# The first feed-forward of a four-layer perceiver: seven program blocks made one, weights quantised as one tile, transposes turned four to a bank and copied by ScalarE

## The chip, the cores and the metric

The kernel runs on one core of a Trainium2 chip (trn2). The metric is the device time of one execution in microseconds (us). Before the change the median of three runs is 4526.8 us.

## The reference, cut to what matters

Twelve stages (cross attention, attention and a feed-forward network, four times over) each add to `x`, of shape (16, 64, 128): 1024 rows of 128 values. The change touches the third stage alone, in which rows and weights are rounded to a 4-bit float grid in groups of 16, each with its own scale:

```python
def fp4_quant_dequant(x):
    xb = x.reshape(shape[:-1] + (shape[-1] // 16, 16))
    scale = jnp.maximum(jnp.max(jnp.abs(xb), axis=-1, keepdims=True) / 6.0, 1e-12)
    xn = xb / scale
    idx = jnp.searchsorted(_MID, jnp.abs(xn))
    return (_GRID[idx] * jnp.sign(xn) * scale).reshape(shape)
...
gate = fp4_linear(x, w_gate)      # w_gate, w_up: (352, 128)
y = fp4_linear(x, w_up)
h = jax.nn.silu(gate) * y         # (rows, 352)
return fp4_linear(h, w_down)      # w_down: (128, 352)
...
x = x + _L0_ffn_ref(_layernorm(x, axis=-1), L0_ffn_w_gate, L0_ffn_w_up, L0_ffn_w_down)
```

`fp4_linear` quantises both of its operands and multiplies them.

## The kernel before

Each stage is a function, and `perceiver` calls the twelve one after the other. A stage is written as program blocks (`nc.Block()`): in a block each engine has a list of instructions of its own, ordered against the other engines by semaphores, and all engines meet in a barrier at the block's end. After a stage `end_stage` lets GpSimd (POOL) clear every semaphore that the stage used and raise it by one again; GpSimd does this alone, ahead of its part of the next stage's first block, while the other engines go on to that block.

`x` lies in SBUF as 8 row tiles of 128 rows by 128 values (NT is 8). `layernorm` is one block: SyncE (SP) issues the stage's loads (`loads`, line 157) and waits for them; VectorE (DVE) makes `c.xn`; TensorE (PE) and ScalarE (ACT) make a transposed copy; GpSimd fills what stands in `fills` (line 168). The block ends when all of that is done.

`stage_l0_ffn`, the feed-forward, is seven blocks before the change:

1. `layernorm`, with seven loads: the gate and up weights in three pieces each (128, 128 and 96 rows by 128 values), and the down weights (128 by 352).
2. `quantize_all` of the rows (128 by 1024), the down weights (128 by 352) and the six pieces. `quantize` is 13 VectorE instructions, each of which waits for the one before it through `Link`.
3. `turn_all` of 17 tiles: TensorE transposes one tile into one of two PSUM buffers (line 236), VectorE copies it out (line 243).
4. For each row tile `t` two matmuls of 352 columns (lines 2887 and 2888) into `pg` and `pu`, two buffers each; ScalarE takes Silu of `pg` (line 2895), VectorE multiplies it with `pu` (line 2901) into `h`.
5. `quantize_all` of `h` (128 by 2816).
6. `turn_all` of the 24 tiles of `h`.
7. The down projection, 24 matmuls into `py` (line 2912), and one addition to `x` (line 2918).

A float32 matmul stands as two instructions in the profile, a transpose as one.

Of the kernel before, what the change touches and what calls it, by code (L numbers as in the profile page):

```python
# [5 lines left out]
ALU = mybir.AluOpType  # L6
ACT = mybir.ActivationFunctionType
# [7 lines left out]
B, S, D = 16, 64, 128  # L15
NT = B * S // 128
# [11 lines left out]
ONE = 1  # L28
# [77 lines left out]
def bc(ap, shape):  # L106
    return ap.to_broadcast(shape)
# [115 lines left out]
def turn_all(c, jobs):  # L223

    nc = c.nc
    with ExitStack() as st:
        pt = [c.ps(st, f"turn{j}", [128, 512]) for j in range(2)]
        turned, copied = c.sem("turned"), c.sem("turn_copied")
        with nc.Block() as block:
            @block.tensor  # L230
            def _(pe):
                for n, (out, src) in enumerate(jobs):
                    if n >= 2:
                        pe.wait_ge(copied, n - 1 + ONE)
                    p, f = src.shape
                    pe.transpose(pt[n % 2][0:f, 0:p], src, c.ident[0:p, 0:p]).then_inc(turned, 1)

            @block.vector
            def _(dve):
                for n, (out, src) in enumerate(jobs):  # L240
                    p, f = src.shape
                    dve.wait_ge(turned, n + 1 + ONE)
                    dve.tensor_copy(out, pt[n % 2][0:f, 0:p]).then_inc(copied, 1)
                dve.wait_ge(copied, len(jobs) + ONE)
# [2574 lines left out]
def quantize(dve, link, v, a, q, b, s, r):  # L2819

    shape = list(v.shape)
    ai, qi, vi = a.bitcast(I32), q.bitcast(I32), v.bitcast(I32)
    link(dve.tensor_reduce(s[:, :, 0], v, X, ALU.max, apply_absolute_value=True))
    link(dve.tensor_scalar(s, s, 1.0 / 12.0, 0.5e-12, ALU.mult, ALU.max))
    link(dve.reciprocal(r, s))
    link(dve.tensor_tensor(v, v, bc(r, shape), ALU.mult))
    link(dve.tensor_scalar(ai, vi, 0x7FFFFFFF, None, ALU.bitwise_and))
    link(dve.tensor_scalar(qi, ai, 0x7F800000, None, ALU.bitwise_and))  # L2830
    link(dve.scalar_tensor_tensor(out=q, in0=q, scalar=0.25 - 2.0 ** -23, in1=a, op0=ALU.mult, op1=ALU.add))
    link(dve.tensor_scalar(qi, qi, 0x7FC00000, None, ALU.bitwise_and))
    link(dve.tensor_scalar(b, a, 0.5, -2.0, ALU.is_gt, ALU.add))
    link(dve.scalar_tensor_tensor(out=b, in0=a, scalar=1.5, in1=b, op0=ALU.is_gt, op1=ALU.add))
    link(dve.scalar_tensor_tensor(out=q, in0=q, scalar=2.0, in1=b, op0=ALU.max, op1=ALU.add))
    link(dve.scalar_tensor_tensor(out=vi, in0=vi, scalar=SIGN, in1=qi, op0=ALU.bitwise_and, op1=ALU.bitwise_or))
    link(dve.tensor_tensor(v, v, bc(s, shape), ALU.mult))


def stage_l0_ffn(c):  # L2840
    nc, d = c.nc, c.dram
    I = 352
    IC = [(0, 128), (128, 128), (256, 96)]
    with ExitStack() as st:
        wT = c.sb(st, "wT", [128, 2, I])
        wdT = c.sb(st, "wdT", [128, 3, D])
        h = c.sb(st, "h", [128, NT, I])
        u = c.sb(st, "u", [128, NT, I])
        a = c.sb(st, "a", [128, NT * I // 16, 16])
        q = c.sb(st, "q", [128, NT * I // 16, 16])  # L2850
        b = c.sb(st, "b", [128, NT * I // 16, 16])
        s = c.sb(st, "s", [128, NT * I // 16, 1])
        r = c.sb(st, "r", [128, NT * I // 16, 1])
        xqT = c.sb(st, "xqT", [128, NT, 128])
        hT = c.sb(st, "hT", [128, 3, NT, 128])
        w = c.sb(st, "w", [128, 2, 3, D])
        wd = c.sb(st, "wd", [128, I])
        wl = [(w[0:n, g, k, :], d[name][o:o + n, :]) for g, name in enumerate(("L0_ffn_w_gate", "L0_ffn_w_up"))
              for k, (o, n) in enumerate(IC)]
        layernorm(c, wl + [(wd[:], d["L0_ffn_w_down"])])  # L2860

        def quantize_all(parts):
            order = c.sem("quant_order")
            with nc.Block() as block:
                @block.vector
                def _(dve):
                    link = Link(dve, order)
                    for v in parts:
                        p, n = v.shape[0], v.shape[1]
                        quantize(dve, link, v, a[0:p, 0:n, :], q[0:p, 0:n, :], b[0:p, 0:n, :], s[0:p, 0:n, :], r[0:p, 0:n, :])  # L2870

        quantize_all([c.xn[:].rearrange("p t (n b) -> p (t n) b", b=16), wd[:].rearrange("p (n b) -> p n b", b=16)]
                     + [v.rearrange("p (n b) -> p n b", b=16) for v, _ in wl])
        turn_all(c, [(xqT[:, t, :], c.xn[:, t, :]) for t in range(NT)]
                 + [(wT[:, g, o:o + n], w[0:n, g, k, :]) for g in range(2) for k, (o, n) in enumerate(IC)]
                 + [(wdT[0:n, k, :], wd[:, o:o + n]) for k, (o, n) in enumerate(IC)])
        with ExitStack() as s2:
            pg = c.ps(s2, "pg", [128, 2, 512])
            pu = c.ps(s2, "pu", [128, 2, 512])
            made, silu, used = c.sem("made"), c.sem("silu"), c.sem("used")  # L2880
            with nc.Block() as block:
                @block.tensor
                def _(pe):
                    for t in range(NT):
                        if t >= 2:
                            pe.wait_ge(used, t - 1 + ONE)
                        pe.matmul(pg[:, t % 2, 0:I], xqT[:, t, :], wT[:, 0, :], start=True, stop=True)
                        pe.matmul(pu[:, t % 2, 0:I], xqT[:, t, :], wT[:, 1, :], start=True, stop=True
                                  ).then_inc(made, 1)

                @block.scalar
                def _(act):
                    for t in range(NT):
                        act.wait_ge(made, t + 1 + ONE)
                        act.activation(u[:, t, :], pg[:, t % 2, 0:I], ACT.Silu).then_inc(silu, 1)

                @block.vector
                def _(dve):
                    for t in range(NT):
                        dve.wait_ge(silu, t + 1 + ONE)  # L2900
                        dve.tensor_tensor(h[:, t, :], u[:, t, :], pu[:, t % 2, 0:I], ALU.mult).then_inc(used, 1)
                    dve.wait_ge(used, NT + ONE)
        quantize_all([h[:].rearrange("p t (n b) -> p (t n) b", b=16)])
        turn_all(c, [(hT[0:n, k, t, :], h[:, t, o:o + n]) for k, (o, n) in enumerate(IC) for t in range(NT)])
        py = c.ps(st, "py", [128, NT, D])
        summed, added = c.sem("summed"), c.sem("added")
        with nc.Block() as block:
            @block.tensor
            def _(pe):
                for t in range(NT):  # L2910
                    for k, (o, n) in enumerate(IC):
                        last = pe.matmul(py[:, t, :], hT[0:n, k, t, :], wdT[0:n, k, :], start=(k == 0), stop=(k == 2))
                last.then_inc(summed, 1)

            @block.vector
            def _(dve):
                dve.wait_ge(summed, 1 + ONE)
                dve.tensor_tensor(c.x[:], c.x[:], py[:], ALU.add).then_inc(added, 1)
                dve.wait_ge(added, 1 + ONE)


BIG = 1.0e30
# [189 lines left out]
def align(c, dcol, dist):  # L3112
# [8 lines left out]
    with ExitStack() as st:  # L3121
# [300 lines left out]
        with nc.Block() as block:  # L3422
# [57 lines left out]


STAGES = [stage_l0_xattn, stage_l0_attn, stage_l0_ffn, stage_l1_xattn, stage_l1_attn, stage_l1_ffn, stage_l2_xattn,
          stage_l2_attn, stage_l2_ffn, stage_l3_xattn, stage_l3_attn, stage_l3_ffn]

# [34 lines left out]
```

## Time and profile before

| | us |
|---|---|
| median of three runs (4524.62 to 4530.95) | 4526.8 |
| the profiled execution's own time | 4532.81 |
| its span in the trace | 4531.1 |
| busy in the span: TensorE matmul | 3534.2 |
| VectorE | 3437.9 |
| ScalarE | 2802.6 |
| GpSimd | 1035.8 |

Span is from the first to the last recorded event of the profiled execution; every time in the rows below counts from its start. The changed stage takes from 557.7 us to 680.1 us in it. The busy sums are over twelve stages that follow one another, so they say nothing about one stage.

### The profile page before, as it was taken

What the parts mean: (1) busy time and instruction counts of PE and PEld (TensorE: products, weight loads), DVE (VectorE), ACT (ScalarE), POOL (GpSimd) and SP (SyncE); (2) the same over time, 40 slices, a digit from 0 to 9 for tenths busy, and PEclk for the clock granted to TensorE, in tenths of its full rate; (3) what the DMA queues carried; (4) which work ended last, traced back from release to release, by engine and by line L of the source; (5) the groups of instructions that cost most, each with busy time, mean ns of one, the idle gap of its engine ahead of it and who ended that gap; (6) DMA issues with size and microseconds to landing.
All of it is one profiled execution on the core that took longest, in us unless ns stands there. A gap on an engine that the chain in (4) does not pass through costs nothing. (4 is left out here: it accounts for less than half of the span.)

```text
span 4531.1 us, 71930 instructions
## 1 busy us (share of the span) xinstructions
PE 3534.2 (78%) x25855; PEld 2837.7 (63%) x25855; DVE 3437.9 (76%) x5581; ACT 2802.6 (62%) x4626; POOL 1035.8 (23%) x1054
## 2 busy tenths in 40 slices
PE   6345638999999677999999875777777777777786
PEld 3334316999998555899999752555555555555574
DVE  4775776777777622877788657999999999999643
ACT  3113505666666423666666534999989998999732
POOL 0000402111210201121111001444444344443310
PEclk9556758999999888999999987999999999999887
DMA  8652001101100101010010001000000000000000
GB/s 273 95 97 67 6 0 64 44 31 37 37 30 16 26 24 62 30 44 30 30 39 28 22 5 39 15 15 21 24 15 15 15 30 15 15 15 8 20 4 17
DMA packets 186565, 161.25 MB, mean 36 GB/s; under 512 B 8220, under 2 KB 174316, under 8 KB 186220
## 3 DMA queue, kind: packets, MB, share of 16 engines
q1 hardware_dynamic: 182828, 142.83, 11.9%
q10 hardware_dynamic: 3392, 13.93, 0.9%
q8 instruction: 203, 3.33, 0.3%
q14 instruction: 142, 1.16, 0.1%
HBM read 127.36 MB, written 20.20 MB: 33 GB/s over the span
## 5 line engine op out<-in xcount | busy, mean ns | idle before, releaser
L538 PEld LDWEIGHTS psU<-ctxN,ST 128*128 128x128 f32 x6656 | 853.8, 191 | 98.1 <-issue 39.2
L538 PE MATMUL psU<-ctxN,ST 128*128 128x129 f32 x6656 | 868.0, 275 | 20.5 <-issue 20.5
L1160 DVE MAX8 top<-pairs 128x8 f32<-128x801 f32 (+1 forms) x512 | 709.2, 1406 | 4.5
L624 ACT ACTIVATE ST<-ST 128x512 f32<-128x512 f32 (+1 forms) x832 | 513.2, 625 | 166.8 <-DVE ST L726 162.5
L1125 POOL TENSOR_TENSOR P<-P,EX 128x1601 f32<-128x1601 f32 x128 | 459.8, 3592 | 580.0 <-ACT P L1035 580.0
L935 PE MATMUL psU<-ctxN,PT 128*128 128x129 f32 (+1 forms) x3328 | 432.6, 281 | 202.5 <-ACT PT L1043 202.5
L726 DVE TENSOR_TENSOR ST<-ST,psB 128x512 f32<-128x512 f32 (+1 forms) x832 | 556.2, 677 | 3.2 <-PE psB L557 3.2
L712 DVE TENSOR_TENSOR psA<-psA,ST 128x512 f32<-128x512 f32 x640 | 446.7, 698 | 136.8 <-ACT ST L616 69.7
L935 PEld LDWEIGHTS psU<-ctxN,PT 128*128 128x128 f32 (+1 forms) x3328 | 395.0, 193 | 226.8 <-ACT PT L1043 226.8
L1165 DVE MATCH_REPLACE8 pairs<-top,pairs 128x801 f32<-128x801 f32 (+1 forms) x384 | 482.3, 1256 | 0.0
L913 PE MATMUL psS<-KT,stat 128*128 128x512 f32 (+1 forms) x1024 | 387.5, 522 | 15.9 <-DVE pairs L1144 15.1
L526 PE MATMUL psS<-statL,ctxH 128*128 128x512 f32 x832 | 392.1, 471 | 6.3 <-ACT ST L616 2.9
L616 ACT ACTIVATE ST<-psS,key_bias 128x512 f32<-128x512 f32 (+1 forms) x416 | 284.2, 683 | 145.0 <-PE psS L526 140.0
L619 ACT ACTIVATE ST<-psS 128x512 f32<-128x512 f32 (+1 forms) x416 | 246.9, 593 | 166.2 <-PE psS L526 160.7
L923 PE MATMUL psT<-ident,P 128*128 128x128 f32 (+1 forms) x1664 | 256.6, 283 | 96.2 <-ACT KT L987 71.2
L526 PE MATMUL psS<-statH,ctxH 128*128 128x512 f32 x832 | 330.5, 397 | 0.0
L526 PE MATMUL psS<-statH,ctxL 128*128 128x512 f32 x832 | 327.3, 393 | 0.0
L913 PEld LDWEIGHTS psS<-KT,stat 128*128 128x128 f32 x1024 | 189.3, 195 | 210.2 <-issue 209.3
L923 PEld LDWEIGHTS psT<-ident,P 128*128 128x128 f32 (+1 forms) x1664 | 192.5, 144 | 166.5 <-ACT KT L987 85.4
L656 POOL CAST ctxH<-ctxM 128x1601 fp32r<-128x1601 f32 x30 | 45.7, 1523 | 1011.1 <-DVE ctxM L685 1011.1
L1043 ACT ACTIVATE PT<-psT 128x512 f32<-128x512 f32 (+1 forms) x512 | 240.6, 510 | 18.5 <-PE psT L923 18.5
L994 ACT ACTIVATE SS<-psS 128x1601 f32<-128x1601 f32 x128 | 192.4, 1503 | 73.7 <-PE psS L913 73.2
(509 smaller groups left out, 6294.8 us busy)
## 6 DMA issues: line engine op xcount, KB each, us to landing
ctxT<-ctxT_scratch SPq DMA_DIRECT2D x48, 800.5 KB, 4.6
ctxN<-in_ctx SPq DMA_DIRECT2D x48, 768.0 KB
ctxT_scratch<-trn ACTq DMA_DIRECT2D x16, 800.5 KB
nat<-in_ctx SPq DMA_DIRECT2D x16, 768.0 KB
dist_scratch<-dd SPq DMA_DIRECT2D x8, 800.5 KB
skewed<-in_ctx SPq DMA_DIRECT2D x8, 768.0 KB
ctx_late<-in_ctx SPq DMA_DIRECT2D x8, 768.0 KB
room<-skewed SPq DMA_DIRECT2D x28, 201.0 KB, 4.2
```

Of the source, the lines that this page charges most:

```text
L526: last = pe.matmul(psS[:, i % RING, :], x[:, u // 2 % 2, o:o + 128], q[:, p % 2, heads, queries], start=(n_pass == 0), stop=(n_pass == 2))
L538: last = pe.matmul(psU[:, q, 0:D + 1], ST[0:n, i % SLOTS, q * 128:q * 128 + 128], ctxN[0:n, j, k, 0:D + 1], start=(k == 0 and q % 2 == 0), ...
L616: act.activation(ST[0:n, i % SLOTS, :], psS[0:n, i % RING, :], ACT.Identity, bias=key_bias[0:n, col:col + 1]).then_inc(copied, 1)
L624: act.activation(ST[0:n, i % SLOTS, :], ST[0:n, i % SLOTS, :], ACT.Exp).then_inc(exp_done, 1)
L712: dve.tensor_tensor(psA[:], psA[:], cell, ALU.max).then_inc(folded, 1)
L726: dve.tensor_tensor(cell, cell, psB[0:n, :], ALU.subtract).then_inc(shifted, 1)
L913: last = pe.matmul(psS[:, o:o + w], stat[:, b % 2, 2 * n:2 * n + 2, :], KT[:, b % 2, o:o + w], start=True, stop=True)
L923: last = pe.transpose(psT[0:w, j, (k % 4) * 128:(k % 4) * 128 + 128], P[:, t % 2, o:o + w], c.ident[:])
L935: last = pe.matmul(psU[:, 0:D + 1], PT[0:w, t % 2, k, :], ctxN[0:w, t // TB % 2, k, 0:D + 1], start=(k == 0), stop=(k == NC - 1))
L1125: pool.tensor_tensor(P[:, j, :], P[:, j, :], EX[:, j, :], ALU.mult).then_inc(p_ready, 1)
L1160: dve.max(top[:, j, 8 * n:8 * n + 8], pairs[:, j, 0:width]).then_inc(listed, 1)
L1165: dve.match_replace(pairs[:, j, 0:width], top[:, j, 8 * n:8 * n + 8], pairs[:, j, 0:width], LOW).then_inc(listed, 1)
```

## The change

`stage_l0_ffn` becomes two blocks, `layernorm` and one for all the rest. The gate, up and down weights are loaded into one tile `w` of 128 by 1120 values and quantised by a single call of `quantize`; GpSimd first fills the 32 unused partitions of two pieces with zeros. The rows are quantised in two halves of four row tiles, the gated rows `h` in two halves as well. Transposes go four to a PSUM bank, and ScalarE copies a bank out in one instruction (line 2934 of the changed kernel). `pu` gets four banks. `py` takes the banks of `pg`. The down projection and the addition are made in halves.

```diff
--- before.py
+++ after.py
@@ -2841,82 +2841,138 @@
     nc, d = c.nc, c.dram
     I = 352
     IC = [(0, 128), (128, 128), (256, 96)]
+    PIECES = 6
+    HALF = NT // 2
+    OPS = 13
+    WEIGHTS, ROWS_A, ROWS_B, HIDDEN_A, HIDDEN_B = (OPS * (n + 1) for n in range(5))
+    TURN_USES = [("w", 0), ("w", 1), ("w", 2), ("x", 0), ("x", 1)] + [("h", n) for n in range(6)]
+    turn_use = {use: n for n, use in enumerate(TURN_USES)}
     with ExitStack() as st:
-        wT = c.sb(st, "wT", [128, 2, I])
-        wdT = c.sb(st, "wdT", [128, 3, D])
+        w = c.sb(st, "w", [128, PIECES * D + I])
+        wT = c.sb(st, "wT", [128, PIECES + 3, 128])
         h = c.sb(st, "h", [128, NT, I])
         u = c.sb(st, "u", [128, NT, I])
-        a = c.sb(st, "a", [128, NT * I // 16, 16])
-        q = c.sb(st, "q", [128, NT * I // 16, 16])
-        b = c.sb(st, "b", [128, NT * I // 16, 16])
-        s = c.sb(st, "s", [128, NT * I // 16, 1])
-        r = c.sb(st, "r", [128, NT * I // 16, 1])
+        a, q, b = (c.sb(st, n, [128, HALF * I // 16, 16]) for n in "aqb")
+        s, r = (c.sb(st, n, [128, HALF * I // 16, 1]) for n in "sr")
         xqT = c.sb(st, "xqT", [128, NT, 128])
         hT = c.sb(st, "hT", [128, 3, NT, 128])
...
+        pieces = w[:, 0:PIECES * D].rearrange("p (g k d) -> p g k d", g=2, d=D)
+        layernorm(c, [(pieces[0:n, g, k, :], d[name][o:o + n, :])
+                      for g, name in enumerate(("L0_ffn_w_gate", "L0_ffn_w_up")) for k, (o, n) in enumerate(IC)]
+                  + [(w[:, PIECES * D:], d["L0_ffn_w_down"])],
+                  [(pieces[IC[2][1]:128, g, 2, :], 0.0) for g in range(2)])
+
+        pt = c.ps(st, "turn", [128, 2, 4, 128])
+        pg = c.ps(st, "pg", [128, 2, 512])
+        pu = c.ps(st, "pu", [128, 4, 512])
+        py = pg[:].rearrange("p a (t d) -> p (a t) d", d=D)
+        quantised, turned, copied = c.sem("quantised"), c.sem("turned"), c.sem("turn_copied")
+        made, silu, gated = c.sem("made"), c.sem("silu"), c.sem("gated")
         summed, added = c.sem("summed"), c.sem("added")
+
+        def halved(n):
+            return slice(n * HALF, n * HALF + HALF)
+
         with nc.Block() as block:
             @block.tensor
             def _(pe):
-                for t in range(NT):
+                def turn(use, jobs):
+                    n = turn_use[use]
+                    if n >= 2:
+                        pe.wait_ge(copied, n - 1 + ONE)
+                    for k, src in enumerate(jobs):
+                        last = pe.transpose(pt[0:src.shape[1], n % 2, k, :], src, c.ident[:])
+                    last.then_inc(turned, 1)
+
+                def gate(t):
+                    pe.wait_ge(copied, turn_use["x", t // HALF] + 1 + ONE)
+                    if t >= 2:
+                        pe.wait_ge(silu, t - 1 + ONE)
+                    if t >= 4:
+                        pe.wait_ge(gated, t - 3 + ONE)
+                    flat = wT[:].rearrange("p n d -> p (n d)")
+                    pe.matmul(pg[:, t % 2, 0:I], xqT[:, t, :], flat[:, 0:I], start=True, stop=True)
+                    pe.matmul(pu[:, t % 4, 0:I], xqT[:, t, :], flat[:, 3 * 128:3 * 128 + I], start=True, stop=True
+                              ).then_inc(made, 1)
+
+                def turn_hidden(half):
+                    pe.wait_ge(quantised, (HIDDEN_A, HIDDEN_B)[half] + ONE)
                     for k, (o, n) in enumerate(IC):
-                        last = pe.matmul(py[:, t, :], hT[0:n, k, t, :], wdT[0:n, k, :], start=(k == 0), stop=(k == 2))
-                last.then_inc(summed, 1)
+                        turn(("h", 3 * half + k), [h[:, t, o:o + n] for t in range(NT)[halved(half)]])
+
+                def down(half):
+                    pe.wait_ge(copied, turn_use["h", 3 * half + 2] + 1 + ONE)
+                    pe.wait_ge(silu, NT + ONE)
+                    for t in range(NT)[halved(half)]:
+                        for k, (o, n) in enumerate(IC):
+                            last = pe.matmul(py[:, t, :], hT[0:n, k, t, :], wT[0:n, PIECES + k, :], start=(k == 0),
+                                             stop=(k == 2))
+                    last.then_inc(summed, 1)
+
+                wide = [w[:, n * 128:n * 128 + 128] for n in range(PIECES)] + [
+                    w[:, PIECES * D + o:PIECES * D + o + n] for o, n in IC]
+                pe.wait_ge(quantised, WEIGHTS + ONE)
+                for n in range(3):
+                    turn(("w", n), wide[4 * n:4 * n + 4])
+                pe.wait_ge(quantised, ROWS_A + ONE)
+                turn(("x", 0), [c.xn[:, t, :] for t in range(NT)[halved(0)]])
+                for t in range(NT)[halved(0)]:
+                    gate(t)
+                pe.wait_ge(quantised, ROWS_B + ONE)
+                turn(("x", 1), [c.xn[:, t, :] for t in range(NT)[halved(1)]])
+                for t in range(NT)[halved(1)]:
+                    gate(t)
+                for half in range(2):
+                    turn_hidden(half)
+                    down(half)
+
+            @block.scalar
+            def _(act):
+                def copy(use, out, rows=128, blocks=4):
+                    n = turn_use[use]
+                    act.wait_ge(turned, n + 1 + ONE)
+                    act.activation(out, pt[0:rows, n % 2, 0:blocks, :], ACT.Copy).then_inc(copied, 1)
+
+                def gate(t):
+                    act.wait_ge(made, t + 1 + ONE)
+                    act.activation(u[:, t, :], pg[:, t % 2, 0:I], ACT.Silu).then_inc(silu, 1)
+
+                copy(("w", 0), wT[:, 0:4, :])
+                copy(("w", 1), wT[:, 4:8, :])
+                copy(("w", 2), wT[0:IC[2][1], 8:9, :], IC[2][1], 1)
+                for half in range(2):
+                    copy(("x", half), xqT[:, halved(half), :])
+                    for t in range(NT)[halved(half)]:
+                        gate(t)
+                for half in range(2):
+                    for k, (o, n) in enumerate(IC):
+                        copy(("h", 3 * half + k), hT[0:n, k, halved(half), :], n)
 
             @block.vector
             def _(dve):
-                dve.wait_ge(summed, 1 + ONE)
-                dve.tensor_tensor(c.x[:], c.x[:], py[:], ALU.add).then_inc(added, 1)
-                dve.wait_ge(added, 1 + ONE)
+                link = Link(dve, quantised)
+
+                def grid(v):
+                    n = v.shape[1]
+                    quantize(dve, link, v, a[:, 0:n, :], q[:, 0:n, :], b[:, 0:n, :], s[:, 0:n, :], r[:, 0:n, :])
+
+                def multiply(t):
+                    dve.wait_ge(silu, t + 1 + ONE)
+                    dve.tensor_tensor(h[:, t, :], u[:, t, :], pu[:, t % 4, 0:I], ALU.mult).then_inc(gated, 1)
+
+                grid(w[:].rearrange("p (n b) -> p n b", b=16))
+                for half in range(2):
+                    grid(c.xn[:, halved(half), :].rearrange("p t (n b) -> p (t n) b", b=16))
+                for half in range(2):
+                    for t in range(NT)[halved(half)]:
+                        multiply(t)
+                    dve.wait_ge(gated, HALF * (half + 1) + ONE)
+                    grid(h[:, halved(half), :].rearrange("p t (n b) -> p (t n) b", b=16))
+                for half in range(2):
+                    dve.wait_ge(summed, half + 1 + ONE)
+                    dve.tensor_tensor(c.x[:, halved(half), :], c.x[:, halved(half), :], py[:, halved(half), :], ALU.add
+                                      ).then_inc(added, 1)
+                dve.wait_ge(added, 2 + ONE)
 
 
 BIG = 1.0e30
```

How the instructions stand in VectorE's list, at the place between the rows' and the gated rows' quantisation. Before (`xqT`, `wT` and `wdT` are transposed rows and weights, `turn` a PSUM buffer; this is the end of the first transposes, the multiplications and the start of the quantisation of `h`):

```order
L243 COPY wT<-turn_102 128x96
L243 COPY wdT<-turn_101 128x128
L243 COPY wdT<-turn_102 128x128
L243 COPY wdT<-turn_101 96x128
L229 UNCONDITIONAL_BRANCH
L2897 UNCONDITIONAL_BRANCH
L2901 TENSOR_TENSOR h<-u,pu 128x352 x8
L2881 UNCONDITIONAL_BRANCH
L2865 UNCONDITIONAL_BRANCH
L2825 TENSOR_REDUCE s<-h 128x176
```

And now:

```order
L2836 SCALAR_TENSOR_TENSOR xn<-xn,q 128x512
L2837 TENSOR_TENSOR xn<-xn,s 128x512
L2961 TENSOR_TENSOR h<-u,pu 128x352 x4
L2825 TENSOR_REDUCE s<-h 128x88
L2826 TENSOR_SCALAR s<-s 128x88
L2827 RECIPROCAL r<-s 128x88
L2828 TENSOR_TENSOR h<-h,r 128x1408
```

The copies and the two block ends have left VectorE's list between the two quantisations, and only four of the eight multiplications stand ahead of the first half of `h`.

TensorE's list from the last transposes of `h` to the next stage, before:

```order
L236 MATMUL turn_105<-ident,h 96x128
L236 MATMUL turn_106<-ident,h 96x128
L229 UNCONDITIONAL_BRANCH
L2908 UNCONDITIONAL_BRANCH
L2912 MATMUL py<-wdT,hT 128x128 x24
L2907 UNCONDITIONAL_BRANCH
```

And now, from the last gate matmul:

```order
L2895 MATMUL pu<-wT,xqT 128x352
L2884 MATMUL turn<-ident,h 128x128 x8
L2884 MATMUL turn<-ident,h 96x128 x4
L2908 MATMUL pg<-wT,hT 128x128 x12
L2884 MATMUL turn<-ident,h 128x128 x8
L2884 MATMUL turn<-ident,h 96x128 x4
L2908 MATMUL pg<-wT,hT 128x128 x12
L2876 UNCONDITIONAL_BRANCH
```

Half of the transposes and of the down projection now stand ahead of the second half's.

ScalarE's list in the new block (before, it held only the table load and eight Silu):

```order
L2934 ACTIVATE wT<-turn 128x512 x2
L2934 ACTIVATE wT<-turn 96x128
L2934 ACTIVATE xqT<-turn 128x512
L2938 ACT_TABLE_LOAD
L2938 ACTIVATE u<-pg 128x352 x4
L2934 ACTIVATE xqT<-turn 128x512
L2938 ACTIVATE u<-pg 128x352 x4
L2934 ACTIVATE hT<-turn 128x512 x2
L2934 ACTIVATE hT<-turn 96x512
L2934 ACTIVATE hT<-turn 128x512 x2
L2934 ACTIVATE hT<-turn 96x512
```

Eleven copies have come to ScalarE, and the load of Silu's table stands behind the first copy of the rows.

## Rows read from the trace of the kernel before

**Rows 1.** Stretch: us, busy of PE, PEld, DVE, ACT, POOL, then PEclk, DMA, GB/s.
```profile
557.00:680.00 123.00, 37.22 (x129) 23.28 (x129) 87.72 (x194) 8.16 (x15) 0.00 (x0) 0.56 0.02 5
```

**Rows 2.** Timeline (start, duration, engine, line, operation), VectorE's first quantisation.
```profile
565.15 1.22 DVE L2825 TENSOR_REDUCE s<-xn 128x64 f32<-128x1024 f32 x1 [2.76 <-PEq L153]
...
568.48 0.69 DVE L2829 TENSOR_SCALAR a<-xn 128x1024 int32<-128x1024 int32 x1
...
577.69 0.52 DVE L2825 TENSOR_REDUCE s<-wd 128x22 f32<-128x352 f32 x1
...
583.66 0.29 DVE L2825 TENSOR_REDUCE s<-w 128x8 f32<-128x128 f32 x1
...
605.84 0.29 DVE L2837 TENSOR_TENSOR w<-w,s 96x128 f32<-96x128 f32 x1
```

**Rows 3.** Timeline, gate matmuls, Silu and the last multiplication.
```profile
614.71 1.51 PE L2887 MATMUL pg<-wT,xqT 128*128 128x352 f32 x2 [0.84 <-PEq L229]
614.95 1.28 ACT L2895 ACT_TABLE_LOAD   x1 [51.39 <-PEq L229]
...
617.43 0.46 ACT L2895 ACTIVATE u<-pg 128x352 f32<-128x352 f32 x1 [1.20 <-PE pu L2888]
...
619.78 0.46 ACT L2895 ACTIVATE u<-pg 128x352 f32<-128x352 f32 x1 [1.88 <-PE pu L2888]
...
621.37 0.47 ACT L2895 ACTIVATE u<-pg 128x352 f32<-128x352 f32 x1 [1.13 <-PE pu L2888]
...
622.55 0.46 ACT L2895 ACTIVATE u<-pg 128x352 f32<-128x352 f32 x1 [0.72 <-PE pu L2888]
...
628.17 0.52 DVE L2901 TENSOR_TENSOR h<-u,pu 128x352 f32<-128x352 f32 x1 [0.66 <-ACT u L2895]
```

**Rows 4.** Timeline, first and last instruction of the quantisation of `h`.
```profile
629.22 3.09 DVE L2825 TENSOR_REDUCE s<-h 128x176 f32<-128x2816 f32 x1 [0.53 <-PEq L2881]
...
656.19 3.09 DVE L2837 TENSOR_TENSOR h<-h,s 128x2816 f32<-128x2816 f32 x1
```

**Rows 5.** Timeline, down projection, addition, start of the next stage.
```profile
670.63 7.70 PE L2912 MATMUL py<-wdT,hT 128*128 128x128 f32 x48 [0.84 <-PEq L229]
678.37 1.22 DVE L2918 TENSOR_TENSOR x<-x,py 128x1024 f32<-128x1024 f32 x1 [8.25 <-PE py L2912]
680.07 0.33 SPq L157 DMA_DIRECT2D ST<-in_L_xattn_Wq  x1
```

**Rows 6.** Waits of SyncE's queue, 557 to 566: us in total, times, longest.
```profile
SPq L153 <- DMA wd<-in_L_ffn_w_down: 2.0, 1, 2.0
SPq L153 <- PEq L153: 1.6, 1, 1.6
```

**Rows 7.** Timeline, ScalarE's end in `layernorm`, and GpSimd's fill in the next one.
```profile
562.96 0.60 ACT L212 ACTIVATE xnT<-ln_pt 128x512 f32<-128x512 f32 x1 [0.64 <-PE ln_pt L220]
...
683.32 0.44 POOL L168 MEMSET mask_raw<- 128x256 uint8 x1 [154.71 <-issue]
```

**Rows 8.** Timeline of the stage before: four transposes into a bank, ScalarE's copy.
```profile
547.98 1.06 PE L1445 MATMUL psT<-ident,P 128*128 128x128 f32 x4
...
549.08 0.60 ACT L1542 ACTIVATE PT<-psT 128x512 f32<-128x512 f32 x1 [3.79 <-PE psT L1445]
```

**Rows 9.** Stretches as in the first group; PEclk stands third from the end.
```profile
618.00:620.00 2.00, 2.00 (x4) 1.12 (x4) 0.45 (x1) 0.22 (x1) 0.00 (x0) 0.50 0.00 0
622.00:624.00 2.00, 2.00 (x7) 0.97 (x6) 0.91 (x2) 0.54 (x2) 0.00 (x0) 1.00 0.00 0
672.00:675.00 3.00, 3.00 (x16) 3.00 (x15) 0.00 (x0) 0.00 (x0) 0.00 (x0) 0.50 0.00 0
675.00:679.00 4.00, 3.34 (x30) 3.14 (x28) 0.63 (x1) 0.00 (x0) 0.00 (x0) 0.99 0.00 0
```

**Rows 10.** VectorE groups, 700 to 1000: form, count | busy, mean ns.
```profile
L726 DVE TENSOR_TENSOR ST<-ST,psB 128x512 f32<-128x512 f32 x133 | 89.2, 677 | 0.0
...
L685 DVE TENSOR_SCALAR ctxM<-ctxT 128x1601 int32<-128x1601 int32 x7 | 6.9, 989 | 0.0
```

More of the change, by code:

```diff
@@ L2855, in stage_l0_ffn @@
         hT = c.sb(st, "hT", [128, 3, NT, 128])
[L2856 to L2883, printed above, removed]
-                    for t in range(NT):
[L2885 to L2902, printed above, removed]
@@ L2903, in stage_l0_ffn @@
-        quantize_all([h[:].rearrange("p t (n b) -> p (t n) b", b=16)])
-        turn_all(c, [(hT[0:n, k, t, :], h[:, t, o:o + n]) for k, (o, n) in enumerate(IC) for t in range(NT)])
-        py = c.ps(st, "py", [128, NT, D])
+        pieces = w[:, 0:PIECES * D].rearrange("p (g k d) -> p g k d", g=2, d=D)
[3 more added lines that the diff above has]
+                  [(pieces[IC[2][1]:128, g, 2, :], 0.0) for g in range(2)])
@@ L2909, in _ @@
             def _(pe):
-                for t in range(NT):
-                    for k, (o, n) in enumerate(IC):
-                        last = pe.matmul(py[:, t, :], hT[0:n, k, t, :], wdT[0:n, k, :], start=(k == 0), stop=(k == 2))
-                last.then_inc(summed, 1)
+                def turn(use, jobs):
[5 more added lines that the diff above has]
+                    last.then_inc(turned, 1)
```

## The prediction, made before the changed kernel ran

> **What bounds the kernel now.** I first read the changed stage as a stretch of its own [rows 1]: of 123 us VectorE is busy 87.7, TensorE 37.2, ScalarE 8.2 and GpSimd nothing, and TensorE's granted clock averages 0.56. The page's sums over twelve stages tell nothing here. Then the timeline, engine by engine. The reader is to see that almost nothing runs beside anything else. From 565.15 to 606.13 VectorE quantises alone [rows 2]; 8.6 us of transposes and barriers follow until the gate matmuls start at 614.71; those, with Silu and multiplication, take until 628.69 [rows 3]; VectorE quantises `h` alone from 629.22 to 659.28 [rows 4]; 11.35 us of transposes and barriers lead to the down projection at 670.63, that takes 7.70, the addition 1.22, and the next stage's first load is issued at 680.07 [rows 5]. So each phase is on the path in full, and what the change is worth is the difference of two such chains. I follow the new one from 565.15 on, with durations of these rows.
>
> **Start.** `layernorm` ends late for a reason that the change touches. SyncE had its last load at hand after 2.0 us of waiting and then waited 1.6 us more for the barrier [rows 6], though ScalarE had ended at 563.56 [rows 7]. The one engine without a row there is GpSimd, which clears and raises the semaphores of the stage before. In the next stage it needed 3.25 us (680.07 to 683.32) before its first fill [rows 5, 7], for 20 semaphores, 40 instructions, some 0.08 us each. The attention stage uses 46, which makes 92 instructions and 7.5 us: from about 557.3 to 564.8, just where the barrier opened. GpSimd is the last one, so the two new fills behind its clears lie on the path. The only row of such a fill takes 0.44 us for 256 narrow elements [rows 7]; these are 128 elements each and may overlap. I take 0.35 us for both with their wait, between 0.2 and 1.0. The first quantisation starts at 565.50.
>
> **Quantisation.** The 13 chained instructions take 12.54 us for 1024 values a partition (565.15 to 577.69), 5.97 for 352 (to 583.66), and 3.75 for each of six pieces of 128 (22.50 in all) [rows 2]; for 2816 they take 30.09 (629.22 to 659.28 and the 0.03 to the next start) [rows 4]. The first and the last give 9.79 ns a value and 2.51 us a call. That line gives 5.96 for 352 and 3.76 for 128, so it holds. A call therefore takes 13.48 us for the weight tile (1120), 7.53 for half the rows (512), and 16.30 for half of `h` (1408). Before: 8 calls and 40.98 us, then one of 30.09. Now: 13.48 + 7.53 + 7.53 = 28.54, and 2 x 16.30 = 32.60. That is 9.9 us less. Weights end at 578.98, rows A at 586.51, rows B at 594.04.
>
> **Transposes and copies.** Those of the weights run under rows A, in 7.5 us that VectorE spends anyway. Nine transposes at 1.06 us for four and three copies at 0.60 [rows 8] need under 4. If that cover were gone they would cost those 4. Rows A: transposes from 586.57, at 587.63 the bank is full, copied at 588.27. Those of rows B and of the first half of `h` run under the quantisations of `h`, 16.3 us each, as do gates 4 to 7 and the first half of the down projection. VectorE's 41 copies are gone.
>
> **Gates 0 to 3.** This is the first place where VectorE may wait. At the low clock (0.50, of the two levels the 1.2 GHz one) the first Silu started 2.72 us after the first matmul (614.71 to 617.43) and the next one 2.35 us later; at the granted 1.00 (2.4 GHz) the step was 1.18 (621.37 to 622.55) [rows 3, 9]. The clock came up about 5.5 us after 614.71. Here matmuls start at 588.33. With the same 5.5 us, half-speed work fills until 593.83, 3.9 us of low-clock work are left and take 1.95, so the fourth Silu starts at 588.33 + 5.5 + 1.95 + 0.37 = 596.15, and the fourth multiplication ends at 596.15 + 0.46 + 0.04 + 0.52 = 597.17. Without the wait it would be 594.04 + 1.8 = 595.9. So 1.3 us of stall, and 3.2 if the clock never comes up. Silu's table load, 1.28 us [rows 3], now stands behind the copy and ends at 589.6, before the first bank is ready: hidden. The first half of `h` ends at 597.23 + 16.30 = 613.53; four multiplications 1.8 (0.52 each, a little overlapped); the second half runs from 615.4 to 631.7.
>
> **Tail.** Nothing covers this. Twelve transposes of the second half: two groups of four follow each other at 0.85 us, the third starts at 633.44 and is full at 634.5, copied at 635.1. Then 12 matmuls, 24 instructions. Before, 48 took 7.70 us, at 0.50 until about 675 and at 0.99 afterwards [rows 5, 9], which fits 0.213 us each at the low and 0.107 at the high clock. TensorE has been idle for over 10 us, so it begins low. If the clock rises 5.5 us after the first transpose, at 637.2, ten instructions are slow and fourteen fast: end at 638.95. The last addition, 128 by 512, is between the 0.52 of 352 values and the 1.22 of 1024 [rows 3, 5], 0.69 on the line through them; with 0.04 before it, 639.7. The gap to the next stage's first issue was 0.48 (679.59 to 680.07) and stays one barrier: 640.15.
>
> **Sum.** 680.07 - 640.15 = 39.9 us. The execution's 4532.81 becomes 4492.9. That execution lies 6.0 above the median, so the median becomes 4526.8 - 39.9 = 4486.9. By parts: quantisation 71.1 to 61.1, -9.9; transposes, copies and barriers 19.9 to the 3.5 that stay in view in the tail, -16.4; gates and multiplications 14.5 to 5.1, -9.5; down projection, addition and the step to the next stage 9.4 to 5.0, -4.5; fills +0.35.
>
> **What the clock may do.** The low clock of both TensorE bursts is the open term. The row shows bursts that began at 0.50 and rose 4.4 and 5.5 us later [rows 3, 5, 9]. Kept low throughout, the gates cost 1.95 more and the tail 1.55: a saving of 36.4, 4490.4. Raised after 4.4 us, as in the down projection of before (670.63 to about 675), the gates stall 0.55 less and the tail ends 0.55 sooner: a saving of 41.0, 4485.8.
> The Trainium skill (TensorE: Matmul & The Clock Gate, section "Loop structure matters more than you think") says that matmuls broken up by long waits run cold. This change cuts TensorE's work into more bursts between waits; by that rule alone both bursts stay low, which is the case of 4490.4. The trace of before agrees on the starts of its bursts and not on their ends.
>
> **Rivals.**
> - *The clock stays low in every burst.* For it: 30 us of idle time ahead of the bursts and short bursts. Against: both long bursts of before rose. 4490.4, chance 0.28.
> - *Quantisation loses its faster steps.* Four of the 13 take 0.69 us at 1024 values where the others take 1.22 [rows 2], 0.52 ns a value less. If the halves and the wide tile did not get this, 4 x 4960 x 0.52 ns = 10.3 us: 4497. Against: every shape before had it. Chance 0.05.
> - *Next stage gives it back.* Its first block waits for loads. Were they issued ahead of the changed stage, it would start work no sooner, and the time would be 4526.8. But they are issued from 680.07 on, behind the stage's end [rows 5], and move with it. Chance 0.02.
> - *Slower: VectorE is slowed by its new neighbours.* Before, TensorE and ScalarE rested in the quantisations, now both read and write beside them. It decides from the point where 61.1 us of quantisation grow by 39.9, by 65%; at twice the time the kernel would take 4548. Against: with all engines busy a 128 by 512 step takes 677 ns and a faster one of 1601 values 989 [rows 10], where the undisturbed lines give 0.69 and 0.99 us. Chance 0.02.
>
> **How the numbers follow.** My forecast, with the clock rising in both bursts, has 0.55; its own range is 4483 to 4490. A gain above 42 us, from a cheaper tail or overlap that I counted as spent, has 0.08. Medians of this kernel lie within about 0.2% (9 us; three runs spread over 6.4), so the range is 4479 to 4496: it takes in the low-clock rival and the fastest case with some 3 us of spread, and leaves the other rivals out. Faster by over 0.2%: 0.96; within 0.2%: 0.02; slower: 0.02.
>
> **What would show it.** In the changed profile: calls of 13.5, 7.5, 7.5, 16.3 and 16.3 us; the first at 565.5 rather than 565.15; VectorE waiting for `u` some 1.3 us in all ahead of the first half of `h`; no wait for `pu` or `turn` elsewhere; 7.3 us between the end of the last quantisation and the last addition; the next stage's first issue near 640. It would be wrong if the quantisation calls grow under their neighbours, if TensorE's in-order list holds up a multiplication beyond gate 3, or if later stages' clock ramps fall differently by more than 2 us.

## The result, and the profile after

The changed kernel takes 4483.72 us, the median of 4 runs (4482.4 to 4494.27), against 4526.99 of before (4 runs beside them, 4524.62 to 4530.95): a ratio of 0.9904 [0.9889, 0.9919], 43 us less. A repeat on another occasion gave 4492.49 (5 runs) against 4528.78 (9): 0.9921 [0.9907, 0.9934], 36 us less. The forecast was 39.9.

The profiled execution took 4484.32 us for a span of 4482.6, 48.5 less than that of before. From the page, in answer to the table of before:

```profile
span 4482.6 us, 71801 instructions
PE 3525.9 (79%) x25855; PEld 2832.6 (63%) x25855; DVE 3418.4 (76%) x5489; ACT 2808.6 (63%) x4637; POOL 1033.6 (23%) x1056
```

The changed stage's columns, as in [rows 1] and [rows 9]. The first line is the whole stage, now 85 us wide and not 123; then the gates, the first half's down projection, and last the second half's with its addition:

```profile
557.00:642.00 85.00, 32.90 (x131) 23.94 (x131) 68.95 (x103) 14.38 (x27) 0.34 (x2) 0.63 0.02 7
...
590.00:592.00 2.00, 2.00 (x5) 1.25 (x4) 1.90 (x4) 0.50 (x1) 0.00 (x0) 0.50 0.00 0
592.00:594.00 2.00, 2.00 (x6) 1.20 (x6) 1.90 (x4) 0.76 (x2) 0.00 (x0) 0.78 0.00 0
594.00:596.00 2.00, 2.00 (x9) 1.22 (x8) 1.93 (x5) 0.63 (x2) 0.00 (x0) 1.00 0.00 0
617.00:620.00 3.00, 2.94 (x24) 2.75 (x24) 2.90 (x4) 0.00 (x0) 0.00 (x0) 1.00 0.00 0
634.00:640.70 6.70, 5.98 (x27) 5.25 (x25) 0.00 (x1) 0.79 (x2) 0.00 (x0) 0.50 0.00 0
```

The timeline of the stage (start, duration, engine, line, operation, with the idle time before it and its releaser), which answers to [rows 2] to [rows 5] and [rows 7]:

```profile
558.45 0.68 DVE L175 BATCH_NORM_STATS2 ln_stats<-x 128x6 f32<-128x128 f32 x3 [0.51 <-PEq L1341]
...
565.56 0.34 POOL L168 MEMSET w<- 32x128 f32 x2 [35.28 <-issue]
566.42 1.32 DVE L2825 TENSOR_REDUCE s<-w 128x70 f32<-128x1120 f32 x1 [3.34 <-PEq L153]
...
579.90 0.69 DVE L2825 TENSOR_REDUCE s<-xn 128x32 f32<-128x512 f32 x1
...
587.43 0.69 DVE L2825 TENSOR_REDUCE s<-xn 128x32 f32<-128x512 f32 x1
...
589.22 1.28 ACT L2938 ACT_TABLE_LOAD   x1
589.25 1.54 PE L2894 MATMUL pg<-wT,xqT 128*128 128x352 f32 x2 [0.69 <-ACT xqT L2934]
...
594.96 1.38 DVE L2961 TENSOR_TENSOR h<-u,pu 128x352 f32<-128x352 f32 x3
596.57 0.52 DVE L2961 TENSOR_TENSOR h<-u,pu 128x352 f32<-128x352 f32 x1 [0.23 <-ACT u L2938]
597.12 1.62 DVE L2825 TENSOR_REDUCE s<-h 128x88 f32<-128x1408 f32 x1
...
613.42 1.81 DVE L2961 TENSOR_TENSOR h<-u,pu 128x352 f32<-128x352 f32 x4
...
615.27 1.62 DVE L2825 TENSOR_REDUCE s<-h 128x88 f32<-128x1408 f32 x1
...
617.02 2.94 PE L2908 MATMUL pg<-wT,hT 128*128 128x128 f32 x24 [0.68 <-ACT hT L2934]
...
631.60 2.89 PE L2884 MATMUL turn<-ident,h 128*128 128x128 f32 x12 [11.64 <-DVE h L2837]
...
635.17 5.49 PE L2908 MATMUL pg<-wT,hT 128*128 128x128 f32 x24 [0.68 <-ACT hT L2934]
640.70 0.69 DVE L2973 TENSOR_TENSOR x<-x,pg 128x512 f32<-128x512 f32 x1 [8.43 <-PE pg L2908]
641.87 0.33 SPq L157 DMA_DIRECT2D ST<-in_L_xattn_Wq  x1
```

The reader is to see one chain on VectorE with hardly a gap: a call's start is the end of the one ahead of it, from 566.42 to 596.34 and from 597.12 to 631.58. TensorE's and ScalarE's work now lies beside it. VectorE waits for them in two places only, 0.2 us for `u` and 8.4 for the tail. The 3.3 us ahead of the first call are the barrier of `layernorm`, which the profile puts down to TensorE's sequencer (PEq); `e_clear_later` below shows who was last. In these lines stand the total, the number of waits and the longest:

```profile
DVE x L2973 <- PE pg L2908: 8.4, 1, 8.4
DVE s L2825 <- PEq L153: 3.3, 1, 3.3
...
DVE h L2961 <- ACT u L2938: 0.2, 1, 0.2
```

From the first statistics instruction to that of the next stage (below: *the stage*) it is 83.5 us, and was 122.4: 38.9 less. The other 9.6 of the 48.5 us between the spans lie in the other stages (4399.2 against 4408.7), 8.6 of them in three whose code is the same: the one right behind (824.1 to 821.7), the longest (1549.4 to 1547.0) and the last attention (155.3 to 151.5).

### The profile page after: what moved, and what is told of

Its sections match the earlier page's. It is cut to its first block and busy times, and to the rows that moved or that the text cites. A ratio compares the mean times of both kernels' runs of the same rounds, so it can differ in the third digit from the quotient of the medians.

```text
span 4482.6 us, 71801 instructions
## 1 busy us (share of the span) xinstructions
PE 3525.9 (79%) x25855; PEld 2832.6 (63%) x25855; DVE 3418.4 (76%) x5489; ACT 2808.6 (63%) x4637; POOL 1033.6 (23%) x1056
```

## The experiments

Theory A: the stage's own chain is the whole gain, by the terms of the prediction. Theory B: the stages around it gain a few us too. The length of the stage tests A's terms one by one; the sum of all other stages, over many kernels, tests B. The stage of the two kernels repeats to 0.05 and 0.2 us, while whole times of one kernel scatter by some 10 us, so terms are read from the stage.

**The two kernels again.**

> The kernel before, unchanged, for a second profile. Stage length is counted from the first statistics instruction (L175) of the feed-forward to that of the next stage: 122.36 us in the first profile, 83.46 with the change, so the stage itself gives 38.9 of the 48.5 us between the two profiled spans. Theory A, the other 9.6 us are scatter between executions: the feed-forward takes 122.4 again, and the other stages together differ from the first profile's 4408.7 us by several us. Theory B, the change lowers later stages: the other stages come out at 4408.7 within 1 us, and those of every kernel with the change near 4399.

> The changed kernel, unchanged, for a second profile and a narrower ratio. Theory A (scatter): feed-forward 83.5 us within 0.3, other stages together anywhere between 4396 and 4409; ratio 0.990 to 0.9915, for 39 to 44 us. Theory B (later stages gain): other stages within 1 us of 4399.1 and a ratio at or below 0.9900.

Measured: 122.3 and 83.2 us in the stage, 4410.3 and 4401.4 elsewhere. The stage repeats; the difference elsewhere is 8.9 us again in these two executions, but see `e_zero_dve` and `e_whole`. Of the three stages named above, the last attention (152.9 against 155.9) and the longest (1547.5 against 1549.4) were shorter again; the one right behind was not (824.7 against 824.1).

**Zero fills by VectorE.** `layernorm` gets `zeros` in place of `fills`:

```diff
+                for out in zeros:
+                    dve.memset(out, 0.0).then_inc(xn_ready, 1)
```

> The two zero fills move from GpSimd to VectorE, behind the normalisation. If GpSimd is the last engine at the barrier of the layernorm block (its fills ran 7.1 us after the stage's start), the first quantisation starts 0.5 to 0.6 us sooner, 7.4 us after the first statistics as in the kernel before, and the feed-forward takes 82.9 us. If the load or ScalarE set that barrier, nothing changes: 83.5 us.

Measured: 82.90 us. The first quantisation starts 7.40 us after the first statistics, as before the change, and 7.97 in the changed kernel:

```profile
564.79 1.32 DVE L2827 TENSOR_REDUCE s<-w 128x70 f32<-128x1120 f32 x1 [2.38 <-PEq L153]
```

The two fills behind GpSimd's clears cost 0.57 us. The other stages took 4407.6, as in the old form.

**Semaphores cleared later.** The 46 semaphores of the attention stage are cleared behind the block of `layernorm` (the added line stands in `stage_l0_ffn` after its call):

```diff
-            c.end_stage()
+            c.end_stage(later=stage is stage_l0_attn)
...
+        c.clear(c.owed)
```

> GpSimd clears and raises the attention stage's 46 semaphores after the layernorm block instead of ahead of it, beside VectorE's first quantisation. If those 92 instructions set the barrier's time, it opens when ScalarE is done, 1.3 to 1.6 us sooner, and the feed-forward takes about 82.0 us. If the loads set it, 83.5 us.

Measured: 81.33 us, 2.1 less than the changed kernel. GpSimd's fills move from 7.1 us behind the first statistics to 0.3 (timeline of `e_clear_later`):

```profile
554.22 0.87 DVE L181 BATCH_NORM_STATS2 ln_stats<-x 128x6 f32<-128x128 f32 x4 [0.51 <-PEq L1347]
554.49 0.34 POOL L174 MEMSET w<- 32x128 f32 x2 [29.41 <-POOLq L1347]
...
560.49 1.32 DVE L2831 TENSOR_REDUCE s<-w 128x70 f32<-128x1120 f32 x1 [1.64 <-PEq L159]
```

SyncE's wait for the barrier falls from 2.5 us to 0.7. The prediction's reading, that GpSimd without a single row holds the barrier, is shown: 1.69 us of the start are its clears and the fills behind them. The other 0.4 us have another source: in this execution TensorE's clock rose sooner in the gates, so that VectorE never waited for `u`, and the tail's 24 instructions took 5.38 us.

**One weight tile in the kernel before.** All weights in `all_w`, one call in place of seven, nothing else:

```diff
-        quantize_all([c.xn[:].rearrange("p t (n b) -> p (t n) b", b=16), wd[:].rearrange("p (n b) -> p n b", b=16)]
-                     + [v.rearrange("p (n b) -> p n b", b=16) for v, _ in wl])
+        quantize_all([c.xn[:].rearrange("p t (n b) -> p (t n) b", b=16), all_w[:].rearrange("p (n b) -> p n b", b=16)])
```

> The kernel before with one edit: all weights in one tile, zero-filled by GpSimd, and one quantisation of 1120 values in place of seven. By the line of 2.51 us a call and 9.79 ns a value, quantisation falls from 40.98 to 26.02 us and the fills add 0.6: feed-forward 108.0 us. Rival, the cost goes by values and partitions and not by calls: 122.4 us or nearly so.

Measured: 107.51 us, 14.8 less than before; whole time 4518.96 (10 runs), ratio 0.9977 [0.9967, 0.9986]. The line of 2.51 us a call holds: the weights' one call runs from 579.82 to 593.27, 13.45 us (its first and last instruction):

```profile
579.82 1.32 DVE L2825 TENSOR_REDUCE s<-w 128x70 f32<-128x1120 f32 x1
...
591.94 1.33 DVE L2837 TENSOR_TENSOR w<-w,s 128x1120 f32<-128x1120 f32 x1
```

**Transposes four to a bank in the kernel before.** Two banks, one copy each by ScalarE (`e_banks_one`) or VectorE (`e_banks_dve`), still in blocks of their own:

```diff
-        turn_all(c, [(hT[0:n, k, t, :], h[:, t, o:o + n]) for k, (o, n) in enumerate(IC) for t in range(NT)])
+        turn_banks([(hT[0:n, k, t:t + 4, :], [h[:, t + j, o:o + n] for j in range(4)])
+                    for k, (o, n) in enumerate(IC) for t in (0, 4)])
```

> The kernel before with one edit: transposes grouped up to four to a bank and copied out by ScalarE, in the same separate blocks, so without overlap. The form alone: 17 and 24 transposes in 7 and 6 groups at 0.6 to 0.9 us a group save 2 and 4 us: feed-forward 116.5 us. So of the 16.4 us that the prediction booked for transposes, copies and barriers the larger part would be overlap and gone barriers. Rival, ScalarE's wide copies bring all of it: 106 us; or nothing: 122.4.

> As e_banks_one (112.1 us feed-forward: the kernel before with transposes up to four to a bank, separate blocks), but VectorE makes the copies. If the gain of 10.3 us comes from the form, fewer and wider copies behind transposes that follow each other, the stage takes 112 to 113.5 us, since a copy of 512 values is 0.69 us on VectorE against 0.60. If ScalarE itself brings it, about 118.

Measured: 112.07 us with ScalarE, where 116.5 was expected, and 112.26 with VectorE; whole time of the first 4520.48 (10 runs), 0.9982 [0.9972, 0.9992]. Of the 10.3 us the two blocks of transposes give 7.2 (8.58 to 6.03 and 11.35 to 6.70). The other 3.1 are in code that the edit does not touch: gates 0.95, down projection 7.70 to 5.59. The timeline of TensorE in `e_banks_one`, the second block of transposes and the down projection:

```profile
654.64 4.25 PE L2884 MATMUL turn<-ident,h 128*128 128x128 f32 x20 [32.16 <-PEq L2864]
...
660.81 5.59 PE L2936 MATMUL py<-wdT,hT 128*128 128x128 f32 x48 [1.10 <-PEq L2876]
```

The granted clock (third from the end) over the same stretch:

```profile
654.00:658.00 4.00, 3.36 (x16) 3.00 (x16) 0.11 (x1) 1.63 (x3) 0.00 (x0) 0.50 0.00 0
658.00:661.00 3.00, 1.72 (x12) 1.03 (x11) 0.00 (x0) 1.85 (x4) 0.00 (x0) 0.95 0.00 0
661.00:666.00 5.00, 5.00 (x46) 5.00 (x46) 0.00 (x0) 0.00 (x0) 0.00 (x0) 1.00 0.00 0
```

And in the kernel before, within its second block of transposes:

```profile
665.00:668.00 3.00, 2.49 (x8) 1.28 (x8) 1.64 (x8) 0.00 (x0) 0.00 (x0) 0.50 0.00 0
```

Here 24 transposes in fours brought the clock to 0.95 within the block, and the down projection began at 1.00; one at a time, with a copy between them, they left it at 0.50 until 675 [rows 9]. In `e_banks_dve` the down projection took 5.60 us. So what TensorE does just ahead of a burst can change the burst's cost, but does not settle it: in the changed kernel the same twelve transposes in fours stand ahead of both halves of the down projection, one of which took 2.94 us and the other 5.49. That ScalarE copies is worth 0.2 us.

**Rows and `h` whole.** The block form of the change without its halves:

```diff
-                for half in range(2):
-                    grid(c.xn[:, halved(half), :].rearrange("p t (n b) -> p (t n) b", b=16))
+                grid(c.xn[:].rearrange("p t (n b) -> p (t n) b", b=16))
```

> The changed kernel with rows and gated rows quantised whole (1024 and 2816 values) instead of in halves, all else kept. Overlap theory: two calls fewer save 5.0 us, but all eight gates come into view (about 10.7 us more) and the whole of the second transposes and down projection (about 6 more): feed-forward 95 us. Rival, the halves are worth nothing beyond their calls' fixed cost: 78.5 us.

Measured: 95.64 us; whole time 4504.28 (4 runs), 0.9938 [0.9921, 0.9954]. Two calls fewer save 5.0 us of VectorE, and 12.2 are lost all the same, since its waits come back (VectorE's waits, 550 to 655: total, times, longest):

```profile
DVE x L2971 <- PE pg L2908: 13.3, 2, 8.7
DVE h L2961 <- ACT u L2938: 12.2, 8, 5.2
```

**The tail's clock.** 18 matmuls without a use, into a bank of `pu` that is free, between the first half's down projection and the second half's transposes:

```diff
-                for half in range(2):
-                    turn_hidden(half)
-                    down(half)
+                turn_hidden(0)
+                down(0)
+                pe.wait_ge(gated, NT + ONE)
+                keep_busy(18)
+                turn_hidden(1)
+                down(1)
```

> 18 matmuls of 352 columns with an unused result stand on TensorE between the first down projection and the second half's transposes, under VectorE's last quantisation. Clock theory: TensorE then enters the tail at 2.4 GHz, the 24 down instructions take 2.9 us instead of 5.5 and the transposes about 0.9 less; feed-forward 80.0 us. Rival, the tail is set by latencies and copies and not by the clock: 83.5 us, or more if the extra matmuls run low themselves and are still going when VectorE is done (up to 10 us more).

Measured: 82.11 us; whole time 4484.45 (4 runs), 0.9898 [0.9883, 0.9913]. The mechanism is as expected, the size is not (timeline of TensorE):

```profile
615.73 5.04 PE L2913 MATMUL pg<-wT,hT 128*128 128x128 f32 x24 [0.68 <-ACT hT L2942]
620.60 10.81 PE L2901 MATMUL pu<-wT 128*128 128x352 f32 x36
631.25 1.04 PE L2884 MATMUL turn<-ident,h 128*128 128x128 f32 x8
...
633.87 2.94 PE L2913 MATMUL pg<-wT,hT 128*128 128x128 f32 x24 [0.68 <-ACT hT L2942]
```

The tail's 24 instructions take 2.94 us and not 5.49. But the first half's took 5.04 here, where the changed kernel had 2.94, so the filler ended late and held up the transposes by 1.0 us. The other 1.1 us of the miss lie ahead of all that, where the code is that of the changed kernel: the gates ran longer at the low clock, and VectorE waited for `u` twice (total, times, longest):

```profile
DVE h L2969 <- ACT u L2946: 1.4, 2, 0.7
```

**Both bursts.** 4 such matmuls ahead of the rows' transposes and 15 ahead of the tail:

```diff
+                pe.wait_ge(copied, 3 + ONE)
+                keep_busy(4)
```

> The changed kernel with unused matmuls ahead of both TensorE bursts that VectorE waits for: 4 between the weights' transposes and the rows', and 15 (not 18, which ran on 1.0 us too long) ahead of the second half's transposes. Clock theory: tail shorter by 3.3 us, wait for Silu gone (0.35 us): feed-forward 79.6 us. If the earlier gain of 1.2 us was all there is: 82.

Measured: 79.67 us, whole time 4485.47 (one run). With 15 the filler ends 0.6 us ahead of the transposes, and the tail's down projection is at the high clock (timeline):

```profile
631.50 2.94 PE L2913 MATMUL pg<-wT,hT 128*128 128x128 f32 x24 [0.68 <-ACT hT L2944]
```

**All together.** Both fillers, zeros by VectorE, semaphores cleared later:

> The three findings together: unused matmuls as in e_busy_both, zero fills by VectorE, the attention stage's semaphores cleared later. If they add, feed-forward 79.6 - 2.0 = 77.6 us, 5.7 less than the changed kernel, and a ratio to the kernel before of 0.989 to 0.991. If later stages scatter by their clock as in all profiles so far, the whole time varies by about 10 us between executions all the same.

Measured: 80.65 us, 3 more than expected; whole time 4482.52 (4 runs), 0.989 [0.9873, 0.9906]. In this execution the first half's down projection ran at the high clock, so the filler ended early, and TensorE was idle for 2.75 us (timeline):

```profile
627.16 1.09 PE L2893 MATMUL turn<-ident,h 128*128 128x128 f32 x8 [2.75 <-DVE h L2845]
...
629.95 5.49 PE L2922 MATMUL pg<-wT,hT 128*128 128x128 f32 x24 [0.68 <-ACT hT L2953]
```

The stretches around it, clock third from the end:

```profile
625.00:627.00 2.00, 0.00 (x0) 0.00 (x0) 1.97 (x2) 0.00 (x0) 0.00 (x0) 1.00 0.00 0
627.00:629.00 2.00, 1.59 (x12) 1.24 (x12) 0.79 (x2) 1.09 (x2) 0.00 (x0) 0.97 0.00 0
630.00:632.00 2.00, 2.00 (x9) 2.00 (x10) 0.00 (x0) 0.00 (x0) 0.00 (x0) 0.50 0.00 0
```

The clock fell behind that gap although transposes were running again. A filler of fixed length after a burst of varying length can be late or too early; the 0.6 us of `e_busy_both` did no harm. The last kernel ties it to VectorE's progress instead:

```diff
-                keep_busy(15)
+                for step, n in ((4, 1), (5, 1), (6, 2), (7, 1), (8, 1), (9, 2), (10, 2), (11, 2), (12, 2)):
+                    pe.wait_ge(quantised, HIDDEN_A + step + ONE)
+                    keep_busy(n)
```

> As e_best, but the unused matmuls ahead of the second half's transposes are paced by VectorE's own steps: one or two behind each of the last ten steps of its last quantisation, so that they end with it whichever clock the first down projection ran at. In e_best the 15 matmuls ended at 625.0 us, TensorE then rested until 627.2, and the down projection ran at 0.50 (5.49 us, feed-forward 80.65 instead of 77.6). Clock theory: with no such rest the tail runs at 1.00, down projection 2.9 us, feed-forward 77.9 us and 5.5 less than the changed kernel; ratio to the kernel before about 0.989. If the low clock of e_best's tail had another cause, 80.5 us again.

Measured: 77.99 us; whole time 4481.91 (4 runs, 4478.17 to 4483.4) against 4532.8 (7): 0.9886 [0.987, 0.9903]. Its timeline shows gaps of 0.21 us and a fast tail:

```profile
625.08 1.45 PE L2910 MATMUL pu<-wT 128*128 128x352 f32 x4 [0.21 <-DVE h L2844]
626.74 1.09 PE L2893 MATMUL turn<-ident,h 128*128 128x128 f32 x8 [0.21 <-DVE h L2845]
...
629.40 2.94 PE L2922 MATMUL pg<-wT,hT 128*128 128x128 f32 x24 [0.68 <-ACT hT L2955]
```

Its stage is 5.2 us shorter than the shorter of the changed kernel's two. The whole time is best here, but its interval overlaps that of the changed kernel's first comparison: such an interval is some 7 us wide to either side, so a gain of 5 us is shown by the stage alone. Against `e_busy_both` the stage gains 1.68 us, which is the earlier start (6.28 us after the first statistics and not 7.96). What pacing shows is a fast tail behind a first half's down projection of 2.94 us, where the fixed filler of `e_best` had lost the clock.

## Why the prediction was right, and which terms were off

The forecast (a saving of 39.9 us, 4486.9) held by its mechanism: every phase was on the path, and the saving is the difference of the two chains. The stage gave 38.9; the two whole-time comparisons, 36 and 43, lie on both sides of it. Term by term, the stage measured from its first statistics:

- *Quantisation.* Forecast 61.1 us, measured 61.15: calls of 13.48, 7.53, 7.53, 16.30 and 16.31. The rivals "loses its faster steps" and "slowed by its neighbours" are refuted: with TensorE and ScalarE at work beside it no call took more than 0.01 us longer than its line.
- *Fills.* 0.35 forecast, 0.57 measured, inside its bounds of 0.2 and 1.0. The cause, GpSimd's clears, is shown by `e_clear_later`.
- *Gates and multiplications.* 5.1 forecast, 4.0 measured, since the clock rose about 3.6 us after the first gate matmul (589.25; a mean of 0.78 over 592 to 594 puts the step at 592.9) and not 5.5: the stall for `u` is 0.2 us and not 1.3. That is the luck of an execution and no property of the change: in `e_busy_tail`, with the same code up to there, the clock rose 6.1 us after the first gate matmul and the stall was 1.4.
- *Transposes and copies.* Forecast hidden but for 3.5 us in the tail; measured 3.6, and no wait of VectorE elsewhere.
- *Tail.* The step "the clock rises 5.5 us after the first transpose, ten instructions are slow and fourteen fast" failed: 0.50 to the end, 5.49 us for the 24 instructions and not 3.8, 10.3 between the last quantisation and the next issue and not 8.45. It was low for all or nearly all of these instructions in the four executions that have this tail and no filler (5.49, 5.47, 5.49 and 5.38 us). `e_busy_both` and `e_best_paced` show that the clock is the cause: kept high, they take 2.94. The price at the low clock was short too: 24 instructions at 0.213 us give 5.1, and they took 5.49.

So 0.2 and 1.9 us too little cost and 1.1 too much, 1.0 in all: the sum is closer than its terms, because two misses on the clock partly cancel. The rival "the clock stays low in every burst" held in one burst of two. By the Trainium skill (TensorE: Matmul & The Clock Gate, section "Loop structure matters more than you think") matmuls with a long DMA wait between each and the next run cold. The waits here are for VectorE and ScalarE. The tail agrees (11.64 us of idle time ahead of it, 0.50 throughout), the gates only at their start: TensorE had idled 5.3 us ahead of the rows' transposes, and the gates began at 0.50, but then the clock rose within them.

Where the saving comes from, by kernels that make one part alone: the weight tile 14.8 us, four transposes to a bank 10.3, the halves within the block 12.2 (`e_whole` against the changed kernel). Their sum is 37.3 of the 38.9; each is one execution's stage, and where the clock rises moves a stage by up to about 1 us. Whole times bear the parts out only roughly: by the ratios the weight tile gives 10 us (6 to 15), the banks 8 (4 to 13), and `e_whole` 28 (21 to 36) where its stage gives 26.7. The prediction gave transposes, copies and barriers 16.4 and the halves no sum of their own; the calls of the weights gain 14.8 and not the 9.9 of quantisation as a whole because the halves cost two further calls, 5.0 us.

"The next stage gives it back" is refuted: the stage right behind took 821.7 and 824.7 us in two executions of the changed kernel and 824.1 in both of before, so at most 0.6 us come back there. Theory B, that stages around gain, is not shown. In executions of the changed form the other stages took from 4396.1 to 4414.4 us, of the old form 4404.1 to 4410.3. The means, 4402.8 (nine kernels) and 4407.3 (five), are 4.4 apart, within the groups' own spreads of 18 and 6 us. The granted clock goes with it: the last attention stage, the same code everywhere, took 153.4 to 157.1 us in the old form, and in the new one from 147.0 (`e_best`) to 159.9 (`e_whole`), with 151.5 in the changed kernel. Stretches of that stage with the same 3816 instructions of TensorE, first in the kernel before:

```profile
4284.00:4439.00 155.00, 132.28 (x3816) 115.25 (x3816) 66.82 (x162) 51.38 (x91) 21.52 (x58) 0.86 0.06 17
```

In the changed kernel:

```profile
4240.00:4392.00 152.00, 129.82 (x3816) 113.28 (x3816) 67.08 (x163) 51.92 (x92) 21.47 (x58) 0.89 0.06 18
```

And in `e_whole`:

```profile
4257.00:4417.00 160.00, 135.18 (x3816) 118.19 (x3816) 66.79 (x162) 51.58 (x91) 21.46 (x58) 0.85 0.06 17
```

VectorE and ScalarE are equally busy in all three; only the clock column and TensorE's time differ. Open stays why it differs between executions, and whether those 4 us follow from the change.

## What to carry to other kernels

When a stage's engines take turns, put the operation with the fixed cost per call on as few calls as give the others something to start on: one call for what nobody waits for early, halves for what feeds the next engine. Two calls more cost 5.0 us here and bought 17.2 of overlap. Before a short TensorE burst on the path, read the granted clock of that burst and what the engine did just ahead of it; filler matmuls that end late hold the burst up, and an idle gap of 2.75 us behind them lost the clock again, so tie them to the progress of the engine that the burst waits for. An engine without a row in a stretch may still be the last at a barrier.

## What the runs showed of the hardware

- GpSimd's clears and increments of semaphores have no rows in any view, yet take time: in the changed kernel its fills came 7.1 us after the stage's first statistics, behind 92 such instructions, and 0.3 us after it when these were moved: about 0.07 us each.
- TensorE's granted clock fell behind a gap of 2.75 us in `e_best`, and stayed at 1.00 across gaps of 0.21 us in `e_best_paced` and of 0.63 us in `e_busy_both`.
- The same instructions after the same work met different clocks in different executions: the first half's down projection took 2.94 us in the changed kernel and in `e_best`, 5.04 in `e_busy_tail`, where nothing ahead of it in the stage differs from the changed kernel.
- The clock rose within a block of 24 fp32 transposes that went out in fours (`e_banks_one`, `e_banks_dve`), and not within one of 24 that went out one at a time (before). Twelve in fours were followed by 1.00 in the changed kernel's first half and by 0.50 in its second, so the form alone does not bring the clock; why it came in the one and not in the other stays open.
